# GpSimd's gathers in a two-layer graph kernel: one short clear ahead of each gather, and one gate per block in place of ten or eleven

## What is computed

```
# layer 0 (edge_attr: 16 numbers per edge)
ew     = (edge_attr @ W_e + b_e).reshape(E, 16, 16)
msg    = einsum('ei,eio->eo', x[src], ew)
neigh  = segment_sum(msg, dst) / max(count, 1) + bias
x      = layernorm(x + neigh)
# layer 1 (edge_type: one of 8)
msg    = einsum('emh,eh->em', edge_emb[type].reshape(-1, 16, 16), x[src])
m      = segment_sum(msg, dst)
h_new  = GRU cell of (m, x)
x      = layernorm(x + h_new)
```

## Time and profile before

| | us |
|---|---|
| median of 3 runs | 5807.87 |
| lowest and highest | 5798.56 and 5818.69 |
| the profiled execution | 5833.2 |
| its span, first to last instruction | 5831.4 |
| TensorE busy in the span | 5227.1 (90%) |
| VectorE busy | 4199.3 (72%) |
| ScalarE busy | 3891.8 (67%) |
| GpSimd busy | 3412.9 (59%) |

### The profile page before, as it was taken

One profiled execution on the slowest core, in us unless ns is written; L12 is line 12 of the kernel. 1 busy time (PEld: TensorE's weight loads), 2 busy tenths in 40 slices (PEclk: granted clock), 3 DMA queues, 4 the chain that ended last, 5 costly groups with the idle time before them and its releaser, 6 DMA issues.

```text
span 5831.4 us, 131035 instructions
## 1 busy us (share of the span) xinstructions
PE 5227.1 (90%) x41758; PEld 4693.1 (80%) x41759; DVE 4199.3 (72%) x5387; ACT 3891.8 (67%) x5533; POOL 3412.9 (59%) x3559
## 2 busy tenths in 40 slices
PE   6999999999999999999978888888888888888887
PEld 5888888888888888888767878788877788788887
DVE  7878787778777788777856666666666666666666
ACT  6666676676666666666566666666666666666664
POOL 6555565555555555555555656655655655655554
PEclk9999999999999999999989999999999999998998
DMA  3111111111111111111111111111111111111110
GB/s 66 33 30 31 33 31 31 31 31 33 30 31 33 30 31 33 31 32 31 25 23 23 23 24 23 23 23 22 23 23 23 23 23 22 24 22 23 23 23 14
DMA packets 330970, 161.25 MB, mean 28 GB/s; under 512 B 193244, under 2 KB 330011, under 8 KB 330771
## 3 DMA queue, kind: packets, MB, share of 16 engines
q1 hardware_dynamic: 218224, 130.59, 9.3%
q0 software_dynamic: 112512, 29.03, 6.3%
q10 hardware_dynamic: 160, 0.80, 0.1%
HBM read 157.44 MB, written 2.66 MB: 27 GB/s over the span
## 4 chain that ended last, share of the span: by engine, by line
PE 63%; issue 15%; DVE 12%; another core or an unknown queue 6%; DVEq 4%; ACT 0%; DMA 0%; POOL 0%; SPq 0%; ACTq 0%
PE psN L752 46%; PE psM L789 15%; DVE cand L953 6%; DVEq L997 2%; DVE nodeT L935 2%; DVE z L991 2%; DVE z L959 1%; DVEq L934 1%; DVEq L952 0%; PE psN L893 0%; PE psM L764 0%; DVEq L958 0%; PE psM L773 0%; DVE grp_hot L943 0%
## 5 line engine op out<-in xcount | busy, mean ns | idle before, releaser
L752 PE MATMUL psN<-table_hi,pick 128*128 128x320 f32 (+1 forms) x13670 | 4080.1, 316 | 167.8 <-DVE cand L953 85.3
L752 PE MATMUL psN<-table_lo,pick 128*128 128x320 f32 (+1 forms) x13670 | 3987.4, 308 | 13.7 <-issue 13.7
L752 PEld LDWEIGHTS psN<-table_hi,pick 128*128 128x128 f32 x13670 | 2598.8, 190 | 306.4 <-issue 226.1
L578 ACT ACTIVATE pick<-dist 128x640 fp32r<-128x640 bf16 (+1 forms) x2485 | 1790.5, 784 | 1336.8 <-PE psN L752 852.8
L752 PEld LDWEIGHTS psN<-table_lo,pick 128*128 128x128 f32 x13670 | 2599.6, 190 | 21.6 <-issue 21.5
L500 POOL DMA_INDIRECT z<-in_x,idx x1761 | 1704.4, 968 | 1176.9 <-issue 417.4
L500 POOL DMA_INDIRECT z<-h_rows,idx x1755 | 1682.2, 959 | 1168.3 <-issue 403.7
L570 ACT ACTIVATE dist<-src_mod,neg_node 128x640 bf16<-128x640 uint16 (+1 forms) x2485 | 1972.6, 874 | 3.3 <-DMA src_mod<-src_mod_rows 3.3
L953 DVE TENSOR_TENSOR cand<-psN,grp_hot 128x640 f32<-128x640 f32 (+1 forms) x1492 | 1122.1, 765 | 1061.3 <-PE psN L752 482.7
L991 DVE TENSOR_TENSOR z<-psD,z 128x2048 f32<-128x2048 f32 (+1 forms) x750 | 1367.8, 1824 | 55.6 <-issue 31.5
L789 PE MATMUL psM<-z,onehot 128*32 128x273 f32 (+1 forms) x12500 | 904.4, 345 | 371.4 <-issue 327.0
(11 more groups left out here) (108 smaller groups left out, 734.3 us busy)
## 6 DMA issues: line engine op xcount, KB each, us to landing
src_mod<-src_mod_rows SPq DMA_DIRECT2D x249, 192.0 KB
src_mod<-src_mod_rows SPq DMA_DIRECT2D x248, 160.0 KB
z<-in_x,idx POOLq DMA_INDIRECT x1761
z<-h_rows,idx POOLq DMA_INDIRECT x1755
eab<-in_edge_attr SPq DMA_DIRECT2D x125, 200.0 KB
idx<-in_src SPq DMA_DIRECT2D x250, 12.5 KB
dstb<-in_dst SPq DMA_DIRECT2D x250, 14.0 KB
grp<-src_grp SPq DMA_DIRECT2D x249, 5.5 KB
```

The lines of the kernel that those rows point to most:

```text
L578: act.activation(pick[j][:, CHUNKS[i], 0:hi - lo], dist[i][:, 0:hi - lo], ACT.Relu, bias=1.0, scale=-1.0).then_inc(l["pick_act"], 1)
L752: mm = pe.matmul(rows[:, :, 0:cells.shape[2]], pick[j][:, c, at:at + P], cells, start=(i == 0 and part == 0), stop=(i == TC - 1 and part = ...
```

## The change

All `picked` gates of the gathers are gone; the gate for the sums (`AFTER_SUMS`) and those for `free` and `idx` stay. Ahead of every gather from the second block of each layer on, GpSimd writes zeros to `rest`, the last 192 columns of `dst_mem` (128 partitions). Nothing reads them afterwards. The clear waits for the clear before it (a semaphore `rest` of its own), and the very first one for `s_span`. That makes 2 x 124 x 14 = 3472 clears.

```diff
-AFTER_OWN = ([{5: 0, 6: 1, 7: 2, 8: 3, 12: 5, 13: 6}] * 2, [{6: 0, 7: 1, 10: 3, 11: 4, 13: 5}] * 2)
+AFTER_OWN = ([{}] * 2, [{}] * 2)
 AFTER_SUMS = (9, 8)
-AFTER_LAST = ([{0: 7, 1: 8, 2: 9, 4: 10}] * 2, [{0: 7, 1: 8, 2: 9, 4: 10}] * 2)
+AFTER_LAST = ([{}] * 2, [{}] * 2)
@@
+REST = 192
@@
+        rest = dst_mem[:, BLK - REST:BLK]
+        assert SPAN_AT + ROW * NB <= BLK - REST
@@
-                hot_g=sem(f"l{k}_hot_g"), sel=sem(f"l{k}_sel"),
+                hot_g=sem(f"l{k}_hot_g"), rest=sem(f"l{k}_rest"), sel=sem(f"l{k}_sel"),
@@
             def gathers(k, table):
                 l = L[k]
+                rests = [0]
@@
                             n += 1
+                            if b > 0:
+                                if rests[0]:
+                                    pool.wait_ge(l["rest"], rests[0])
+                                elif k == 0:
+                                    pool.wait_ge(s_span, 1)
+                                pool.memset(rest, 0.0).then_inc(l["rest"], 1)
+                                rests[0] += 1
                             pool.indirect_dma_start(
                                 xs[k][buf][:, g, :], None, table,
                                 bass.IndirectOffsetOnAxis(ap=idx[buf][:, g:g + 1], axis=0),
```

## The result

The changed kernel takes 7592.48 us (median of 4 runs, 7570.64 to 7593.92) against 5805.11 us for the kernel before on the same chip (4 runs, 5798.56 to 5818.69). The ratio is 1.3083, with a 95% interval of 1.306 to 1.3106. The forecast was 5650 us, and the range ended at 5840.

What follows compares the result with a forecast made beforehand. TensorE was taken as the bound, delayed by a backlog of gathers issued every 1.26 us against 1.42. Terms -134 - 31 + 6 = -159 from 5833.2 give 5674, less 25 for the runs' median: 5650 us, range 5530 to 5840.

Steps and rivals of the forecast that it cites:

- the clear's cost: Added time between gathers on GpSimd: taken as 0.25 us, bounded by 0 and 0.55, for a pace of 1.51 us.
- case 4: Rival: the clear is no pause, fourteen gathers run in one row starving TensorE; 2000 us more, chance 5%.
- case 2: Rival: nothing comes of it, sums lose the gain or the clear hides in idle time; 5808 us, 12%.
- the limit of 1.42 us: Each gather blocks TensorE's traffic for part of 1.42 us; a slower pace than that builds up no backlog.
- The forecast's own upper bound, 5740: Upper bound of the forecast case (68%): 5740 us, with half of the term for layer 1.
- Taking them away saves nothing by itself: Gates on GpSimd: removal alone gains nothing, as gathers leave it some 5 us a block to spare.
- -134: Layer 1: both TensorE waits, 1.64 us, go, less 0.56 us of sums' gaps; 1.08 us x 124 blocks.
- -31: Layer 0: TensorE's wait of 0.25 us a block for VectorE goes, over 124 blocks; 31 us less.
- +6: Starts of both layers: block 1's nine gathers lengthen the stall by about 3 us each; 6 us more.
- The sums' own gaps: Layer 1: a third gather beside the sums adds 0.56 us of gaps; in layer 0 gaps stay.
- The clock: TensorE's half-level stretches: cost up to 82 us in layer 1; nothing taken either way.
- Case 3: Rival: GpSimd becomes the bound, a gather taking 1.81 us and a block 25.4 us; 6440 us, 15%.

Runs made afterwards that it cites:

- e8: The changed kernel with clears of 256 columns instead of 192, where the kernel before takes 5802.10 us: 6269.09 us.
- e7: The changed kernel without any clears, so neither picked gates nor clears, where the kernel before takes 5802.10 us: 8101.11 us.
- e9: The changed kernel with clears of 320 columns instead of 192, where the kernel before takes 5794.93 us: 5736.94 us.
- e5: The changed kernel as it is, run again on a chip where the kernel before takes 5802.10 us: 7101.56 us.
- e10: The changed kernel with clears of 400 columns instead of 192, where the kernel before takes 5794.93 us: 5683.07 us.
- e15: The changed kernel with clears of 360 columns instead of 192, where the kernel before takes 5789.11 us: 5551.84 us, ratio 0.9589.
- e2: The changed kernel with clears of 400 columns instead of 192, on the chip where the kernel before takes 4916.07 us: 5639.87 us.
- e16: The changed kernel with clears of 400 columns instead of 192, where the kernel before takes 5789.11 us: 5672.19 us, ratio 0.9796.
- e1: The changed kernel with clears of 256 columns instead of 192, on the chip where the kernel before takes 4916.07 us: 5233.87 us.
- e4: The changed kernel with the earlier gates put back beside the 192-column clears, on the chip where the kernel before takes 4916.07 us: 5134.88 us.
- e14: The changed kernel with each gather fetching 64 rows instead of 128 from the third block on, where the kernel before takes 5789.11 us: 7661.73 us.

## Why the prediction was wrong

**What bounds the kernel: right in kind.** Rows of gathers do delay TensorE's instructions and semaphores, and a slower pace cures it. What was not seen: this belongs to the chip (or to the visit to it) and not to the kernel alone. The kernel before takes 4916 us on one chip and 5800 on others, 880 us apart, where the prediction set out from 154 and 336 us of idle time.

**The step that failed first: the clear's cost.** "I take 0.25 us, its own length", for a pace of 1.51. The clear measured 0.274 us, slightly over the estimate, but it came with 0.14 us on the pace, since 0.30 us of idle time between gathers became 0.16. The two terms are not additive. Pace was 1.40 us, under the 1.42 us that the prediction itself named as the limit ("anything over 0.16 us does that"). The bounds of 0 and 0.55 us held the value; the choice between them did not ask on which side of 0.16 they fall. By its own model every price from 0 to 0.16 us, nearly a third of the span between its bounds, means "still a backlog, and now in longer rows"; only the 5% of case 4 and a part of the 12% of case 2 stood for that.

The Trainium skill (GPSIMD Engine Reference, Instruction dispatch) says that an instruction's completion does not hold the next one on GpSimd back. The prediction worked out from it that a clear would add its columns alone, and the trace agrees: at the 0.76 ns a column of the earlier trace rows, 192 columns are 0.146 us, and 0.14 was measured. From 192 to 400 columns the pace goes up by (1.574 - 1.400)/208 = 0.84 ns a column. The prediction cited the rule, asked only whether GpSimd would become the bound, and wrote that "the sum would stay as it is". It had not held 0.146 against its own 0.16.

**The rows.** "The gathers would then run in rows of nine and five" was wrong as well. The waits for `free` and `idx` were met in time, so the only pause is at the gate for the sums, and the rows have 14 gathers.

**The second: the limit of 1.42 us.** It was read off the spacing of TensorE's starved matmuls, as if that were how long a gather holds TensorE up. e8 at 1.454 us refutes it: 6269 us. Starved matmuls come at multiples of some 0.70 us (e7), so 1.42 looks like two steps of it rather than the time that a gather takes up. The time was least at a pace of 1.54 us, and even there the interference was not gone. At the forecast pace of 1.51 the time is e9's 5737 us. The forecast's own upper bound, 5740, just holds it, and the 5650 is 87 too low. A block of layer 1 takes 22.16 us in e9, as in e6, the kernel before on another chip, where the forecast took 1.08 us off a block; the sums' windows (5.7 and 4.1 us) are no shorter than the kernel before's (5.1 to 5.5 and 4.2 in two traces).

**The gates "cost nothing".** "Taking them away saves nothing by itself" was right as far as GpSimd's time goes. Their price as pauses was left to the clear to pay. e5 and e7 against e6 give it: 8101 - 5798 = 2303 us without any clear, of which 192 columns buy back 1000 on the same chip.

**Layer 1, layer 0 and the starts.** None of -134, -31 and +6 came to be. The start of layer 0 has an 11.14 us wait for "remote", against the 13.87 of the earlier trace rows, and 174 more waits of this kind follow over both layers, up to 9.3 us long. The sums' own gaps, which were to grow, went to nothing, because GpSimd stands still while they run.

**The clock.** It was taken at nothing either way, and about half of the loss lies in TensorE's busy time, at a mean clock of 0.82. A clock term is to be tied to each rival: the case with long stalls has it, the forecast does not.

**The rivals.** Case 4 is what happened: 14 gathers in one row and two matmuls per 1.4 us. The 2000 us it named against 1787 measured were a fair price; its chance of 5% was not. Its reason was only half right: a stand is not the only thing that lets the results out (e9, e10, e15), but this clear was no pause. Case 3 (GpSimd as the bound) did not come at 192 columns on this chip. It is what e2, e10, e15 and e16 show, and e1 and e4 in layer 1.

**What would show it.** Clears of about 0.25 us: 0.274. GpSimd busy 850 us more: 939.6. Starts 1.45 to 1.55 us apart: 1.40, and this line shows the step that failed. VectorE's "remote" waits, to be gone or under 0.7 us, are 689.1 us in all against 355.9 before, the sign that it named for case 4; a block of layer 1, to be near 21.6 us, takes 28.92.

## What to carry to other kernels

When a change aims at a rate, work its size out against the threshold before anything else, and take an instruction's cost as the difference it makes from start to start, since part of it can fall into idle time that was there anyway. Gates that seem to wait for nothing useful may be what keeps a queue short: give each one taken away a price as a pause. And run a kernel on more than one chip before tuning to a delay without a cause in the profile: 360 columns make this kernel 4.1% faster on a chip of the kind of the result's, while on the chip with 4916 us wider clears only cost (256 columns 6.5%, 400 columns 14.7%).

## What the runs showed of the hardware

- The same program takes 4915.78 us on one chip and 8101.11 us on another, at the same pace of gathers and with transfers that are as quick. Gathers from GpSimd's queue delay TensorE's instructions and semaphores on four of the five chips of the experiments, and on that of the result, and not on the fifth. Which resource the gathers and TensorE share there, and what is different on the fifth (the chip itself, or something of that one visit), **was not settled**. Not the bytes or rows (e14); whether it is a gather's 32 packets, its 16 increments of a semaphore or the instruction itself wasn't tried.
- In every profile from an affected chip, those of before and after among them, the profile has no landing time for these gathers; in the four from the other chip it has 2.3 or 2.4 us, in e2 for those of layer 0 only. A missing landing time in both layers is thus a sign of the affected kind that a single profile shows.
- TensorE's starved matmuls start at multiples of about 0.70 us in e7 (1629 of 1929), less clearly in the changed kernel (866 of 1868).
- Wider spacing of the gathers ends the long stalls before it ends the late semaphores: in e15, at 1.54 us, ScalarE learns of the finished sums a median of 2.2 us late, in e10 and e16, at 1.57 us, 1.1 us late, and in e2, on the unaffected chip, 0.04 us after they end.
- A clear directly behind a gather starts with no idle time, and the gather behind it 0.16 us later, where gather to gather has 0.30: 192 columns cost 0.28 us busy and 0.14 us of pace.
- A gather of 64 rows takes 0.92 us on GpSimd against 0.96 for 128: halving its rows saves 0.04 us there.
